# Two halves of 256 tokens instead of one pass of 512: the up product of an expert layer, with each weight tile loaded twice

## The reference

```
group = arange(8) // 2
mid = silu(einsum('keh,ehf->kef', tokens, W_up[group]) + b_up[group])   # 512 -> 1365
out = einsum('kef,efh->keh', mid, W_down) + b_down                      # 1365 -> 512
y   = zeros.at[idx].add(G[..., None] * out)
x   = x + tanh(g_ffn) * y
```

## Time and profile before

| | us |
|---|---|
| median of 3 runs (3065.02 to 3070.32) | 3069.49 |
| the profiled execution, its own time | 3062.04 |
| its span, first to last instruction | 3060.3 |
| PE busy | 2955.4 (97%) |
| DVE busy | 1823.4 (60%) |
| ACT busy | 1130.1 (37%) |

### The profile page before, as it was taken

How to read it: one execution, slowest core, us unless ns; L and a number is a source line. 1 busy time by engine, 2 the same in 40 slices (tenths; PEclk the granted TensorE clock), 3 DMA queues, 4 the chain that set the end, 5 groups by cost and what they waited for, 6 DMA issues and landing times.

```text
span 3060.3 us, 60770 instructions
## 1 busy us (share of the span) xinstructions
PE 2955.4 (97%) x24708; PEld 2398.0 (78%) x24708; DVE 1823.4 (60%) x5124; ACT 1130.1 (37%) x2025; POOL 1064.2 (35%) x1029
## 2 busy tenths in 40 slices
PE   6999999999998599999999999999999999999998
PEld 5888888888886377877777777777787787778886
DVE  6999999999998645354454444544434445444332
ACT  5777788777876311121121121122111112112110
POOL 4777686777766311121122111121112112121111
PEclk9999999999999699999999999999999999999999
DMA  3243434434342421231142231232123214222121
GB/s 130 84 167 113 167 134 147 156 125 168 119 162 89 143 51 34 38 99 31 40 105 38 46 79 34 37 91 67 31 38 86 47 31 111 38 49 58 35 37 24
DMA packets 140062, 250.70 MB, mean 82 GB/s; under 512 B 31456, under 2 KB 31456, under 8 KB 139784
## 3 DMA queue, kind: packets, MB, share of 16 engines
q1 hardware_dynamic: 105784, 170.80, 16.6%
q0 software_dynamic: 28672, 67.65, 12.4%
q10 hardware_dynamic: 5328, 8.36, 0.9%
HBM read 137.23 MB, written 101.19 MB: 78 GB/s over the span
## 4 chain that ended last, share of the span: by engine, by line
PE 63%; DVE 1%; DMA 1%; issue 0%; ACT 0%; POOL 0%; ACTq 0%; DVEq 0%; POOLq 0%
PE DN L1717 32%; PE UP L1688 30%; PE TT L1661 1%; DMA w_raw<-in_L_ffn_W_down 1%; DVE c_hit L1380 0%; PE c_bank L1373 0%; DVE down_lo L1246 0%; PE c_bank L1357 0%; DVE c_hit L1401 0%; ACT z L1631 0%; DVE c_within L1396 0%; ACT down_hi L1240 0%; POOL out_x L1606 0%; DVE c_gained L1433 0%; DVE mid_lo L1749 0%
## 5 line engine op out<-in xcount | busy, mean ns | idle before, releaser
L1606 POOL DMA_INDIRECT out_x<-y,slots x128 | 208.4, 1628 | 1621.8 <-DVE y L1773 1621.8
L1631 ACT ACTIVATE z<-UP,bup 128x512 f32<-128x512 f32 (+1 forms) x352 | 240.6, 686 | 1086.1 <-PE UP L1688 1067.4
L1717 PE MATMUL DN<-down_hi,mid_hi 128*128 128x512 f32 x1408 | 570.6, 405 | 0.0
L1688 PE MATMUL UP<-xT_hi,up_lo 128*128 128x512 f32 (+1 forms) x1408 | 555.5, 395 | 0.0
L1688 PE MATMUL UP<-xT_hi,up_hi 128*128 128x512 f32 (+1 forms) x1408 | 553.9, 393 | 1.5 <-DVE xT_lo L1728 0.9
L1688 PE MATMUL UP<-xT_lo,up_hi 128*128 128x512 f32 (+1 forms) x1408 | 552.0, 392 | 0.0
L1717 PE MATMUL DN<-down_hi,mid_lo 128*128 128x512 f32 x1280 | 505.7, 395 | 0.0
L1717 PE MATMUL DN<-down_lo,mid_hi 128*128 128x512 f32 x1280 | 505.7, 395 | 0.0
L1747 DVE CAST mid_hi<-z 128x512 fp32r<-128x512 f32 (+1 forms) x352 | 151.1, 429 | 487.4 <-ACT z L1631 487.4
L1771 DVE TENSOR_TENSOR y<-DN,bdn 128x512 f32<-128x512 f32 x128 | 88.5, 691 | 432.4 <-PE DN L1717 419.6
L1688 PEld LDWEIGHTS UP<-xT_hi,up_hi 128*128 128x128 f32 (+1 forms) x1408 | 260.3, 185 | 68.4 <-ACT z L1631 3.8
(11 more groups left out here) (264 smaller groups left out, 4961.9 us busy)
## 6 DMA issues: line engine op xcount, KB each, us to landing
xs<-in_x SPq DMA_DIRECT2D x32, 1024.0 KB, 8.2
kraw<-in_ctx SPq DMA_DIRECT2D x32, 1024.0 KB, 5.6
out_x<-xs SPq DMA_DIRECT2D x32, 1024.0 KB, 12.7
rows_scratch<-xfb SPq DMA_DIRECT2D x32, 1024.0 KB, 11.2
w_raw<-in_L_ffn_W_down SPq DMA_DIRECT2D x40, 512.0 KB, 4.3
w_raw<-in_L_ffn_W_up SPq DMA_DIRECT2D x16, 682.5 KB, 4.2
mid_hi<-mid_hi ACTq DMA_DIRECT2D x32, 86.0 KB
mid_lo<-mid_hi ACTq DMA_DIRECT2D x32, 84.0 KB
```

Source lines behind the costliest of these rows:

```text
L1606: pool.indirect_dma_start(out_rows, bass.IndirectOffsetOnAxis(ap=slots[:, m:m + 1], axis=0), y[:, t, :], None, compute_op=ALU.add).then_in ...
L1631: act.activation(z[0:r, k % 2, :], UP[k % 3][0:r, :], ACT.Silu, bias=bup[0:r, e // 2, f:f + 1]).then_inc(s["z"], 1)
L1688: mm = pe.matmul(UP[k % 3][0:r, :], weights.up[wa][:, c, f * P:f * P + r], xT[xa][:, c, :], start=first, stop=(c == CH - 1 and wa == 1))
L1717: mm = pe.matmul(DN[m % 2][:, :], lhs, rhs, start=first, stop=(f == FCH - 1 and lhs is parts[-1][0]))
```

## The change

Each slice of the up product is made in two halves of 256 tokens. The first half goes through all 12 pairs of weights and tokens and writes columns 0 to 255 of the PSUM bank, then the second half goes through the same 12 pairs again and writes columns 256 to 511. Every weight tile is loaded once for each half. The semaphore `up` is raised after the last matmul of the second half, and the wait for `tlo` stands in the first half of the first slice only.

```diff
-                        first = True
-                        for c in range(CH):
-                            if n == 0 and at == 0:
-                                pe.wait_ge(s["tlo"], c + 1)
-                            for wa, xa in ((0, 0), (0, 1), (1, 0)):
-                                mm = pe.matmul(UP[k % 3][0:r, :], weights.up[wa][:, c, f * P:f * P + r], xT[xa][:, c, :],
-                                               start=first, stop=(c == CH - 1 and wa == 1))
-                                first = False
+                        for half in range(2):
+                            cols = slice(half * BLK // 2, (half + 1) * BLK // 2)
+                            first = True
+                            for c in range(CH):
+                                if n == 0 and at == 0 and half == 0:
+                                    pe.wait_ge(s["tlo"], c + 1)
+                                for wa, xa in ((0, 0), (0, 1), (1, 0)):
+                                    mm = pe.matmul(UP[k % 3][0:r, cols], weights.up[wa][:, c, f * P:f * P + r], xT[xa][:, c, cols],
+                                                   start=first, stop=(c == CH - 1 and wa == 1))
+                                    first = False
                         mm.then_inc(s["up"], 1)
```

## The result

The changed kernel takes 3100.16 us (median of 4 runs, 3097.22 to 3100.75) beside 3067.96 us for the kernel before: a ratio of 1.0099, 95% interval 1.0086 to 1.0112, about +30 us. It is slower, as forecast, and inside the range of 3084 to 3205, but by a little over half of the 57 us that the sum gave.

What follows compares the result with a forecast made beforehand. The prediction took PE's own instruction stream to bound the kernel. +161 ns a slice over 352 slices gave +56.8 us, on the median of 3069.5 us 3126 us (+1.9%), range 3084 to 3205.

Steps and rivals of the forecast that it cites:

- the sum: Up product: 24 x 122 = 2928 ns a slice instead of 2767, over 352 slices +56.8 us.
- PE's stream is the time: Expert stage: its time is the length of PE's own instruction stream; anything added lengthens the end one for one.
- the rest costs nothing: Outside the up product's pitch: instruction issue, semaphore, ScalarE, VectorE, DMAs and the down product add no time.
- the pitch of 256 columns: Up product: 122 ns from one half-length matmul to the next, taken from L760; range 119 to 125, 60%.
- the 17.3 ns: Up product: part of the 230.6 ns pitch above 213.3 ns for 512 columns, either fixed or proportional to columns.
- So loading should not set the pitch: Up product: a load's floor of 0.105 to 0.11 us lies under the 122 ns pitch, by some 12 ns.
- Cheap instruction: Rival, up product: most of the 17.3 ns goes with columns; pitch 117 ns, +14.5 us, 3084 us; 14%.
- Faster: Rival, up product: short matmuls lose the 17.3 ns and run at the load floor, 112 ns; -27.8 us, 3042; 4%.
- Collision: Rival, up product: load and stream hinder one another; pitch 131 ns, +133 us, 3202 us; 14%.
- serial load: Rival, up product: each full 188 ns load fits between matmul starts, setting the pitch; +614 us, 3684 us; 3%.
- No change: Rival, up product: all of the 17.3 ns is proportional to columns; pitch 115.3 ns, 3069 us; 5%.

Runs made afterwards that it cites:

- bf16, 512 and 256: High and low parts of up weights and turned tokens in bf16: on the kernel before (512 columns) 3020.01 us, on the changed kernel (256) 3026.53 us.
- one column, 256: The changed kernel with the up product's moving operand a single column read 256 times, loads unchanged: 3048.75 us.
- the longer rows: SBUF rows of the up weights lengthened from 1365 to 1408 words: on the changed kernel 3092.5 us, on the kernel before 3061.43 us.

## Why the prediction was right, and where its size was off

**That PE's stream is the time** held. PE's idle time in the expert stage is 11.0 us before (2011.00 - 1999.97) and 10.1 after, and the end moved with the sum of the slices.

**That halving costs something in the up product, for each matmul,** held, and so did "the rest costs nothing": the down product and the clock are unchanged.

**The size** was 56.8 us where the stage grew by 30.9. The term mis-sized is the pitch of 256 columns: 122 ns, "so the second pair starts 0.122 us after the first". It measured 119.4. 24 x 2.6 ns x 352 = 22 us of the difference of 26, and the rest is the waits that PE lost (2.5 us) and the slices of 85 features (1.3 us). The 122 came from one row, 0.40 us, printed to 0.01 us: half a hundredth on either side is 5 ns, and times 8448 that is 42 us. The forecast's own range of 119 to 125 held it by a hair.

The same trace had the better number. It holds 128 such sets of four. In 127 of them the second pair starts 116 to 123 ns after the first, 119.2 in the mean (the one left out stands at 381 ns); the set of the earlier trace rows has 121. With 119.2 the sum would have been 24 x 119.2 - 2767 = 94 ns a slice, +33 us. That this group resembles the up product so closely was luck, though: the down product in halves has the up product's shapes and takes 113.3.

**How the 17.3 ns divide** is the step that failed in its reasoning: the prediction knew only a fixed part and one proportional to columns, and its 122 came to most of it fixed. The runs divide it otherwise. In ns for 512 columns:

| | before | changed | from |
|---|---|---|---|
| columns | 213.3 | 213.3 | 2.4 GHz |
| instructions, 2.5 each | 2.5 | 5.0 | bf16, 512 and 256 |
| load longer than the stream | 0 | 5.1 | one column, 256: 223.3 |
| reading real 4-byte columns | 14.8 | 15.4 | the rest of 230.6 and 238.8 |

So the part I had suspected of being fixed, the 14.8, goes with the columns. That the load's part and the reading's part simply add in the kernel with real data is this table's assumption, and the slices of 85 features, where the load is too short to bind, don't bear it out. The first matmul of such a slice and the first of the next, in the kernel before (12 matmuls) and in the changed one (24):

```profile
2052.89 0.39 PE L1688 MATMUL UP<-xT_hi,up_hi 128*85 128x512 f32 x1
...
2055.66 0.39 PE L1688 MATMUL UP<-xT_hi,up_hi 128*128 128x512 f32 x1
```

```profile
2076.39 0.28 PE L1690 MATMUL UP<-xT_hi,up_hi 128*85 128x256 f32 x1
...
2079.22 0.28 PE L1690 MATMUL UP<-xT_hi,up_hi 128*128 128x256 f32 x1
```

230.8 ns before, as with full loads, and 117.9 after, 1.5 less than with full loads. So of the 8.2 ns that a pair costs more, 3 go when the load is short, and 5 stay: 2.4 for the second instruction, and the rest, 2 to 3 ns, with the real columns read in two passes. With one column repeated the load's share was 5. The load and the reading of real columns thus seem to hide one another in part. With the longer rows even the 3 ns are not there (117.8 ns with full loads, 117.8 to 120.1 with short ones), so the load's share with real columns is between nothing and 3 ns. Why the reading costs more in two passes, no run shows.

**"So loading should not set the pitch"** nearly held: 119.4 is above the load's floor, which measured 111.7 where the prediction had 105 to 110, and the load adds 1.5 ns to a matmul.

**The rivals.** "Cheap instruction" (117 ns) was right that an instruction costs 2.5 ns and no more, but had no price for the load or for reading real columns in two passes; it forecast +14.5 us. "Faster" was right that there is a floor near 112, and wrong that real data run at it in the up product; in the down product they nearly do (113.3), and there the change of halving is indeed faster. "Collision" at 131 ns and "serial load" at 188 are refuted by 119.4. "No change" by the ratio.

**Left open:** why a pair of halves stands 15.4 ns over the one-column pair in the up product but only 3.4 in the down product (226.7 - 223.3), while at 512 columns both pay about the same for real columns (14.8 and 17.5). The longer rows account for 3.2 of the 15.4, whether by the loaded tile's alignment or not. Whether it is the place of the moving operand in SBUF relative to the loaded one was not tried.

## What to carry to other kernels

- With fp32r operands a load of 128 columns sets a floor to the pitch: 111.7 ns here, for a stream of 128 columns as for one of 256 that reads one column again and again, and 75.6 ns for a load of 85. The transposes of this kernel, whose load rows last 140 ns and not 188, are not bound by it (77.6 ns). At 256 real columns load and stream are about equal, and splitting a pass that is bound by TensorE costs the second instruction and some of that floor. But the same split gained in the down product: try it on the chip for each product.
- When a price is multiplied by thousands, take it from a distance over many repeats, not from one row printed to 0.01 us.
- When a pass is split, look where the small steps that stood inside it come to stand: here a step set too early cost more than the split itself (3111.75 us with it, 3056.32 without).

## What the runs showed that was not expected

- An fp32r matmul of 512 real columns takes 230.6 to 233.3 ns; the same with bf16 parts, or with one column repeated, 215.8. The bf16 version of the up product makes the kernel 1.7% faster, at the price of fewer bits.
- The same halving costs 8.2 ns a pair in one product and gains 6.6 in a dense stretch of the other (3.2 in its mean), in one kernel with the same shapes.
- Rows of 1408 words instead of 1365: 1.6 to 1.7 ns less a matmul in the full slices, at either size, and 2.4 ns more in the slices of 85 features at 512.
- A load of 85 columns instead of 128 brings the floor from 111.7 to 75.6 ns.
